# A graph transformer network of two layers on one core: the experts' shared blocks and combining put in loops, second biases added by VectorE, logits sorted in the norm, edge sums moved behind a range's first group

## The chip, the cores and the metric

One core of one Trainium2 chip runs the whole network as one program. The metric is the device time of one execution in microseconds, here the median of three. The engines are named as the profile names them: PE is TensorE's matmul side and PEld its weight loads, DVE is VectorE, ACT is ScalarE, POOL is GpSimd and SP is SyncE, which issues most of the transfers.

## The reference, cut to what matters

2500 nodes with 256 features and 80,000 directed edges go through two layers. Three pieces matter here.

- Graph convolution in both directions, then a batch norm over nodes: `h_fwd = (segment_sum(x[src], dst) / degree) @ W_l_f.T + b_l_f + x @ W_r_f.T`, `h_bwd` the same with `src` and `dst` exchanged, and the two halves of 128 features side by side.
- Mixture of experts: `shared = gelu(x @ W1s + b1s) @ W2s + b2s`; each row picks its two best of 8 logits `x @ Wr`, with softmax weights `w` normalised over the two; `routed = sum over the two of w * (gelu(x @ W1p[e] + b1p[e]) @ W2p[e] + b2p[e])`; the result is `x + shared + routed`.
- A layer norm stands before each of these stages.

The other parts (Taylor attention, linear attention, the second graph convolution, slice attention) run the same code before and after.

## The kernel before, in words

The rows are T = 20 tiles of P = 128 nodes; X (residual), XN (normed) and XT (normed and transposed) stay in on-chip memory. Every stage is a block in which each engine has its own list of instructions, joined by semaphores; all engines meet between two blocks.

**Graph stage** (`graph_stage`, from line 235). The adjacency matrix is built from one-hot matrices, 80 ranges of 32 target nodes, four ranges (x = 0 to 3) to a strip of 128 (index t). A range is a variable number of groups of four chunks of 128 edges, at least two. Per chunk DVE writes a one-hot of the keys (L505) and for three chunks of four one of the lows (L504); ACT makes the fourth low in two steps (L570, L572); PE multiplies the pair (L691). There are four one-hot buffers, so DVE may be one group ahead of PE. A range's first group stands in front of the hardware loop over the rest of its groups. Behind that loop PE turns five tiles of the strip before (`turn`, L721), sums the forward messages with them (`forward`, L730: 5 matmuls of 257 columns), and in range x = 2 multiplies the strip's own features by the root weights (L710). ACT copies that product to XN (L608), and POOL adds the bias of 256 columns to it tile by tile (L385).

**Backward stage** (`backward_stage`, from line 757). PE sums the backward messages by 7 cuts of up to three tiles (L800), from strips read back from memory. DVE combines the forward half first (`forward_h`, L882), then evacuates cut after cut (L870). PE wants the forward half at its column sums (L807), after the second cut.

**Norm before the experts** (`norm_stage("ln1")`, router given). DVE normalises 20 tiles (L157), PE transposes five blocks of four tiles (L195) into six banks and multiplies each block by the router weights (`route`, L211); all logits go to one bank. SP loads the experts' biases and the first two sets of weights meanwhile.

**Experts stage** (`experts_stage`, from line 1590). DVE copies the 160 logits of a row of partitions (L1850), takes the eight best (L1852) and their indices (L1855) tile by tile, and works out masks, counts, weights and slots. PE counts ranks by two matmuls (L1709, between hidden columns 4 and 5 of block 0). When the slots are known POOL scatters the rows to memory with 40 indirect transfers (L1684), and SP reads them back ordered by expert (L1657). Meanwhile PE computes shared blocks 0 to 2 of 512 rows: `hide`, 8 hidden columns (L1718), ACT the gelu of each (L1814), then `give`, four tiles (L1726), each followed by a matmul of the second biases `b2` with the weights of the experts (L1729, contraction over 9 rows; the weights are turned by L1702 and copied by ACT in L1807), and DVE adds the tile to X (L1881). Block 0 uses six banks for hidden columns, the other blocks two. Then PE transposes the ordered rows (L1781) and the routed tiles run in hardware loops: L1761, gelu L1827, L1767, copied by DVE in L1914 and stored by SP. When all are stored POOL gathers them by 40 indirect transfers (L1689) beside shared blocks 3 and 4, which are written out like 0 to 2, and DVE combines (L1923) and counts the next norm's statistics (L1927) in four runs of five tiles, three of them ahead of block 4's additions.

Of the kernel before, what the change touches and what calls it, by code (L numbers as in the profile page):

```python
# [19 lines left out]
def graph_network(nc, a, out):  # L20
# [44 lines left out]
    with top:  # L65
# [34 lines left out]
        def norm_stage(tag, eps=1e-5, gamma=None, beta=None, counted=0, loads=(), router=None):  # L100
# [9 lines left out]
            s_gb, s_last = sem(tag + "_gb"), sem(tag + "_last_emptied")  # L110
# [13 lines left out]
            with tmp, nc.Block() as block:  # L124
# [9 lines left out]
                def _(dve):  # L134
# [5 lines left out]

                    even, odd = lnst[:, :, 1], lnst[:, :, 4]
# [13 lines left out]
                    for b in range(NB):  # L155
# [3 lines left out]
                        if gb is not None:  # L159
# [4 lines left out]
                            dve.tensor_tensor(blk(XN, b), blk(XN, b), spread(gb[:, 1, :], 1, WT), ALU.add).then_inc(s_affine, 1)  # L164
                    dve.wait_ge(s_tr, NB * CB)
                    dve.tensor_copy(*cols(NB - 1, CB - 1)).then_inc(s_last, 1)

# [23 lines left out]
                def _(pe):  # L191
# [7 lines left out]
                    def route(b):  # L199
                        wr, arrived = router  # L200
# [7 lines left out]
                        NE = wr.shape[-1]  # L208
                        for t in range(b * WT, (b + 1) * WT):
                            for c in range(CB):  # L210
                                pe.matmul(bank[NBANK][:, t * NE:(t + 1) * NE], XT[:, c, t * P:(t + 1) * P], wr[:, c, :], start=c == 0, stop=c == CB - 1)  # L211
# [22 lines left out]
        def graph_stage(keep):  # L234
# [27 lines left out]
            s_rp, s_rc, s_rb = sem("root_product"), sem("root_copied"), sem("root_biased")  # L262
            s_fw, s_fc = sem("forward_summed"), sem("forward_copied")
            with tmp:
# [35 lines left out]
                bl = sb(tmp, "linear_bias", [P, 2 * P])  # L300
                gz = sb(tmp, "z_scale", [P, 3])
                raw = [sb(tmp, f"z_raw{k}", [P, 2, 2 * P]) for k in range(2)]
                zb, AG, back = keep
# [29 lines left out]
                with nc.Block() as block:  # L333
# [26 lines left out]
                    def _(pool):  # L360
# [263 lines left out]
                    def _(pe):  # L624
# [56 lines left out]
                        def window(i, k, x, ranges, load_next):  # L681
# [20 lines left out]
                            t = i * 2 + k  # L702
# [36 lines left out]
        def backward_stage(keep, bn, loads):  # L739
# [3 lines left out]
            zb, AG, back = keep  # L743
# [13 lines left out]
            s_var, s_rt = sem("bn_variance"), sem("bn_root")  # L757
            with tmp:
# [14 lines left out]
                with nc.Block() as block:  # L773
                    @block.sync
                    def _(sp):
# [11 lines left out]
                        sp.wait_ge(s_next, 16 * len(loads))  # L787

# [67 lines left out]
                    def _(dve):  # L856
                        st = Steps(dve, s_ch)

                        def evacuate(j):
# [3 lines left out]
                            dve.wait_ge(s_bk, j + 1)  # L863
                            st.then(dve.tensor_scalar(sd[k][:, 0:n], PS[:, 3 * k:3 * k + n, CNT:CNT + 1].rearrange("p n o -> p (n o)"), 1.0, None, ALU.max))
# [10 lines left out]
                        def forward_h():  # L875
                            st.then(dve.tensor_scalar(indeg[:, :], AG[:, :, CNT:CNT + 1].rearrange("p t o -> p (t o)"), 1.0, None, ALU.max))
# [709 lines left out]
        def experts_stage(held, arrived):  # L1586
# [12 lines left out]
            w1, w2, b1r, b2, _ = held  # L1599
# [12 lines left out]
            with tmp:  # L1612
                hid = sb(tmp, "hidden", [P, FB, W])
                b1 = sb(tmp, "b1_cols", [P, NX * FB])
                lg = sb(tmp, "logits", [P, T, NE])
                top8 = sb(tmp, "top8", [P, T, 8])
                ix = sb(tmp, "top8_index", [P, T, 8], mybir.dt.uint32)
# [5 lines left out]
                eq = [sb(tmp, f"chosen_weight{k}", [P, T, NE]) for k in range(K)]  # L1623
                mk = sb(tmp, "expert_weight", [P, T, NX])
                mkT = sb(tmp, "expert_weight_turned", [NX, NP])
# [16 lines left out]
                with nc.Block() as block:  # L1642
                    @block.sync
                    def _(sp):
# [13 lines left out]
                        sp.wait_ge(s_y, EARLY * WT)  # L1658
# [34 lines left out]
                    def _(pe):  # L1693
# [3 lines left out]
                        def hidden_bank(b, f):  # L1697
                            return bank[f % 6] if b == 0 else bank[f % 2]

                        def turn_weights(b):  # L1700
# [11 lines left out]
                        def hide(b, f, buf):  # L1712
                            if b == 0 and f >= 6:
                                pe.wait_ge(s_g, f - 5)
# [697 lines left out]
```

## Time and profile before

| | us |
|---|---|
| median of 3 executions (2136.07 to 2140.94) | 2137.51 |
| the profiled execution's own time | 2132.05 |
| its span, first to last instruction | 2130.3 |
| PE busy | 1784.7 (84%) |
| PEld busy | 1098.3 (52%) |
| DVE busy | 1084.6 (51%) |
| ACT busy | 831.9 (39%) |
| POOL busy | 260.3 (12%) |

The span is 1.75 us short of the profiled execution's own time. The busy shares are averages over stages with different limits. The mean granted clock of TensorE is 0.929 of its full 2.4 GHz; it stands at full speed or at half. The graph stage takes the first quarter of the span (to 503 us), the experts stage the part from 1008 to 1567 us.

### The profile page before, as it was taken

The numbers are of one execution on the slowest core, as the hardware profiler recorded it, in microseconds if no ns is written. First come the engines' busy times: TensorE is split into PE (matmuls) and PEld (weight loads), VectorE is DVE, ScalarE is ACT, GpSimd is POOL, SyncE is SP. The second block draws the span as 40 slices with busy tenths as digits, with TensorE's granted clock in tenths as the row PEclk, the third lists the DMA queues.
The fourth block names the chain that finished last, engine by engine and source line by source line (L and its number), as shares of the span: only waits on it lengthen the run. The fifth ranks groups of instructions, "written<-read, shape, count | busy, mean of one in ns | idle before, by whom it ended". The sixth has DMA issues, their size and how long they took to land. (4 is left out here: it accounts for less than half of the span.)

```text
span 2130.3 us, 34130 instructions
## 1 busy us (share of the span) xinstructions
PE 1784.7 (84%) x9535; PEld 1098.3 (52%) x9536; DVE 1084.6 (51%) x3108; ACT 831.9 (39%) x1831; POOL 260.3 (12%) x340
## 2 busy tenths in 40 slices
PE   6888888887858999998669999999559857976867
PEld 4234444445636423335437999997244446433436
DVE  7999988886488663334201000000347652334662
ACT  3456777773113475663112444433113233001312
POOL 2000000000092000000510000003300022201102
PEclk9999999999978999998879999999679978987988
DMA  2001111116440000002241112121110001411001
GB/s 73 0 26 60 51 75 75 75 75 212 132 138 1 1 1 1 1 1 81 77 138 40 59 60 96 59 96 56 55 40 0 0 8 67 137 64 31 0 0 51
DMA packets 87011, 117.78 MB, mean 55 GB/s; under 512 B 7404, under 2 KB 73263, under 8 KB 86927
## 3 DMA queue, kind: packets, MB, share of 16 engines
q1 hardware_dynamic: 81614, 105.62, 14.6%
q0 software_dynamic: 3936, 10.37, 1.5%
q8 instruction: 54, 0.88, 0.2%
q10 hardware_dynamic: 1376, 0.66, 0.1%
q14 instruction: 31, 0.25, 0.0%
HBM read 69.75 MB, written 46.87 MB: 55 GB/s over the span
## 5 line engine op out<-in xcount | busy, mean ns | idle before, releaser
L691 PE MATMUL bank<-onehot_key,onehot_low 128*128 128x320 bf16 x1720 | 320.3, 302 | 58.6 <-DVE onehot_key L505 23.4
L505 DVE TENSOR_SCALAR onehot_key<-iota_keys,edge_keys 128x640 bf16<-128x640 f16 x860 | 313.2, 385 | 0.0
L691 PEld LDWEIGHTS bank<-onehot_key,onehot_low 128*128 128x128 bf16 x1720 | 123.2, 97 | 241.6 <-DVE onehot_key L505 216.5
L504 DVE TENSOR_SCALAR onehot_low<-iota_low,edge_low,window_offset 128x128 bf16<-128x128 f16 x645 | 205.8, 319 | 33.0 <-PE bank L691 26.2
L1827 ACT ACTIVATE hidden<-bank,b_cols 128x128 f32<-128x128 f32 x344 | 126.5, 368 | 178.5 <-PE bank L1761 155.2
L1761 PE MATMUL bank<-slot_columns,w 128*128 x1376 | 163.6, 278 | 3.3 <-issue 3.3
L1914 DVE COPY slot_columns<-bank 128x256 f32 x43 | 18.3, 425 | 290.6 <-PE bank L1767 290.6
L1761 PEld LDWEIGHTS bank<-slot_columns,w 128*128 128x128 f32 x1376 | 163.2, 195 | 5.7 <-issue 3.5
L1767 PE MATMUL bank<-w,hidden 128*128 128x256 f32 x688 | 155.6, 379 | 0.0
L1767 PEld LDWEIGHTS bank<-w,hidden 128*128 128x128 f32 x688 | 127.4, 190 | 15.5
L570 ACT ACTIVATE low_distance<-iota_window,edge_low_negated 128x128 f32<-128x128 f32 x215 | 86.6, 403 | 112.0 <-PE bank L691 110.7
L1536 ACT ACTIVATE XT<-bank 128x512 f32<-128x512 f32 x160 | 84.5, 601 | 60.8 <-PE bank L1464 60.8
L1718 PE MATMUL bank<-XT,w 128*128 128x512 f32 x160 | 77.1, 642 | 35.2 <-ACT hidden L1814 34.6
L1881 DVE TENSOR_TENSOR X<-X,bank 128x256 f32<-128x256 f32 x20 | 8.4, 422 | 191.7 <-PE bank L1729 111.3
L1726 PE MATMUL bank<-w,hidden 128*128 128x256 f32 x320 | 79.5, 395 | 24.0 <-issue 20.7
L572 ACT ACTIVATE onehot_low<-low_distance,onesf 128x128 bf16<-128x128 f32 x215 | 86.3, 402 | 7.0
L1033 PE MATMUL bank<-sg_z,sg_strip 128*128 128x512 f16 x400 | 86.5, 379 | 1.5 <-POOL sg_z L962 1.5
L1689 POOL DMA_INDIRECT slot_columns<-slot_results,slots x40 | 38.0, 950 | 404.1 <-SPq L1670 392.2
L1726 PEld LDWEIGHTS bank<-w,hidden 128*128 128x128 f32 x320 | 60.6, 194 | 44.3 <-issue 30.8
L1408 ACT ACTIVATE XT<-bank 128x512 f32<-128x512 f32 x120 | 62.9, 599 | 27.5 <-PE bank L1358 27.5
L1993 PE MATMUL bank<-w_kv,la_cols 128*128 128x512 f32 x160 | 73.0, 601 | 0.0
L1718 PEld LDWEIGHTS bank<-XT,w 128*128 128x128 f32 x160 | 32.7, 209 | 76.2 <-issue 39.7
(475 smaller groups left out, 2870.3 us busy)
## 6 DMA issues: line engine op xcount, KB each, us to landing
AT_dram<-at_strip SPq DMA_DIRECT2D x20, 640.0 KB, 4.0
A_dram<-a_strips SPq DMA_DIRECT2D x20, 640.0 KB, 3.0
sg_strip<-AT_dram SPq DMA_DIRECT2D x20, 640.0 KB, 3.9
back_strip<-A_dram SPq DMA_DIRECT2D x24, 480.0 KB, 7.0
w<-in_L_ffn_W1p SPq DMA_DIRECT2D x8, 1024.0 KB, 4.9
w<-in_L_ffn_W2p SPq DMA_DIRECT2D x8, 1024.0 KB, 7.6
slot_rows<-ty_zero SPq DMA_DIRECT2D x1, 6144.0 KB, 23.7
slot_columns<-slot_rows SPq DMA_DIRECT2D x12, 512.0 KB, 8.9
```

What stands on the lines that cost most here:

```text
L504: dve.tensor_scalar(ohl[:, q, :], iow[:, :], lowc[:, ds(c, 1)], woff[:, ds(w, 1)], ALU.subtract, ALU.is_equal)
L505: dve.tensor_scalar(ohk[:, q, :], ioh[:, :], key[:, ds(c, 1)], None, ALU.is_equal).then_inc(s_key[q], 1)
L570: act.activation(far[:, q - QV, :], wide[:, :], ACT.Square, bias=lows[:, ds(chunk(n, offset, q), 1)]).then_inc(s_sq, 1)
L572: act.activation(ohl[:, QV:Q, :], far[:, 0:Q - QV, :], ACT.Relu, bias=onesf[:, 0:1], scale=-1.0).then_inc(s_low, 1)
L691: last = pe.matmul(bank[2 * (x % 2) + h][:, 0:HB], ohl[:, q, :], ohk[:, q, h * HB:(h + 1) * HB], start=start and q == 0, stop=q == Q - 1, ...
L1033: last = pe.matmul(bank[5 + d % 3][:, :], strips[d % NBUF][:, s, :], zb[:, s, :], start=s == 0, stop=s == T - 1)
L1536: act.activation(FE[:, m % NF, :], bank[m % NS][:, :], ACT.Square).then_inc(p_fa, 1)
L1718: last = pe.matmul(hidden_bank(b, f)[:, :], w1[buf][:, c, f * P:(f + 1) * P], XT[:, c, b * W:(b + 1) * W], start=c == 0, stop=c == CB - 1)
L1726: pe.matmul(bank[2 + j][:, 0:C], hid[:, f, j * P:(j + 1) * P], w2[buf][:, f, :], start=f == 0, stop=False)
L1761: last = pe.matmul(bank[f % 4][:, 0:P], w1[buf][:, c, f * P:(f + 1) * P], XS[:, t, c * P:(c + 1) * P], start=c == 0, stop=c == CB - 1)
L1767: last = pe.matmul(bank[4][:, 0:C], hid[:, f, 0:P], w2[buf][:, f, :], start=f == 0, stop=f == FB - 1)
L1827: act.activation(hid[:, f, 0:P], bank[f % 4][:, 0:P], ACT.Gelu, bias=b1[:, ds((e + 1) * FB + f, 1)]).then_inc(s_rg, 1)
```

## The change

1. Graph stage: for x = 1, 2, 3 the `forward` sums of the strip before are issued behind the range's first group and ahead of the loop over its other groups, no longer behind `turn`; for x = 0 they stay where they were. POOL's bias additions are taken out.
2. Backward stage: POOL adds the backward half of the bias by cuts (7 instructions), for each of which DVE's evacuation waits; DVE adds the forward half in one instruction of 128 x 2560 at the head of `forward_h`.
3. Norm: logits of a block go to one of two banks; DVE copies, sorts and indexes them block by block (`sort`), blocks 0 to 2 ahead of its last copy of XT, blocks 3 and 4 behind it, inside the norm's block.
4. Experts: b2 is loaded to all partitions (9 x 256 values each, where it was 9 rows). The masks of weights, their turning, their copies and the 20 bias matmuls are gone. DVE adds the shared second bias to all of X in one instruction, and each routed tile's second bias as it evacuates it (in a loop over experts around the loop over tiles).
5. Experts: the rank matmuls stand ahead of block 0, behind a wait for the counts. Shared blocks 0 to 2 and 3 to 4 are hardware loops on PE, ACT and DVE with six banks for hidden columns; columns 2 to 5 wait for the additions of the block before, columns 6 and 7 for gelus of this block. Combining is a loop over tiles: add the first, wait, add the second, wait, statistics.

```diff
@@ graph_stage, PE
                             group(before, True)
                             following = load_next()
+                            t = i * 2 + k
+                            if t >= 1 and x:
+                                forward(t - 1, 1 - k, x)
                             with pe.Fori(before + 1, following[0]) as n:
                                 group(n, False)
                             if t >= 1:
                                 turn(t - 1, 1 - k, x)
-                                forward(t - 1, 1 - k, x)
+                                if x == 0:
+                                    forward(t - 1, 1 - k, x)
@@ graph_stage, POOL
-                        for t in range(T):
-                            pool.wait_ge(s_rc, t + 1)
-                            pool.tensor_tensor(XN[:, t, :], XN[:, t, :], bl[:, :], ALU.add).then_inc(s_rb, 1)
@@ backward_stage
+                    @block.gpsimd
+                    def _(pool):
+                        for lo, hi in cuts:
+                            pool.tensor_tensor(part(XN, 1, slice(lo, hi)), part(XN, 1, slice(lo, hi)), spread(bl[:, P:2 * P], 1, hi - lo), ALU.add).then_inc(s_bias, 1)
...
+                            dve.wait_ge(s_bias, j + 1)
...
+                            dve.tensor_tensor(part(XN, 0), part(XN, 0), spread(bl[:, 0:P], 1, T), ALU.add)
@@ norm_stage, DVE
+                    def sort(b):
+                        lg, top8, ix = router[2]
+                        NE = lg.shape[-1]
+                        dve.wait_ge(s_lg, b + 1)
+                        dve.tensor_copy(lg[:, b * WT:(b + 1) * WT, :].rearrange("p t e -> p (t e)"), bank[NBANK + b % 2][:, 0:WT * NE]).then_inc(s_lc, 1)
+                        dve.wait_ge(s_lc, b + 1)
+                        for t in range(b * WT, (b + 1) * WT):
+                            last = dve.max(top8[:, t, :], lg[:, t, :])
+                        st.then(last)
+                        for t in range(b * WT, (b + 1) * WT):
+                            last = dve.max_index(ix[:, t, :], top8[:, t, :], lg[:, t, :])
+                        if b == NB - 1:
+                            st.then(last)
@@ experts_stage, PE
+                        def shared(blocks, buf, arrived, routed_tiles=None):
+                            with pe.Fori(*blocks) as b:
+                                if routed_tiles is not None:
+                                    pe.wait_ge(s_rc, routed_tiles + 1)
+                                pe.wait_ge(s_w[buf], arrived)
+                                for f in range(FB):
+                                    if 2 <= f < 6:
+                                        pe.wait_ge(s_yf, b * WT + (f - 1))
+                                    if f >= 6:
+                                        pe.wait_ge(s_g, b * FB + (f - 5))
+                                    for c in range(CB):
+                                        last = pe.matmul(bank[f % 6][:, :], w1[buf][:, c, f * P:(f + 1) * P], XT[:, c, ds(b * W, W)],
+                                                         start=c == 0, stop=c == CB - 1)
+                                    last.then_inc(s_h, 1)
+                                pe.wait_ge(s_g, b * FB + FB)
+                                for j in range(WT):
+                                    for f in range(FB):
+                                        last = pe.matmul(bank[2 + j][:, 0:C], hid[:, f, j * P:(j + 1) * P], w2[buf][:, f, :],
+                                                         start=f == 0, stop=f == FB - 1)
+                                    last.then_inc(s_y, 1)
...
+                        pe.wait_ge(s_cnt, 3)
+                        pe.wait_ge(s_bt, 1)
+                        for k, m in enumerate((below, onesf)):
+                            last = pe.matmul(bank[6 + k][:, 0:NE * T], m[:, :], cnt[:, :, :].rearrange("p e t -> p (e t)"), start=True, stop=True)
+                        last.then_inc(s_rank, 1)
+                        shared((0, EARLY), 0, 32)
@@ experts_stage, DVE
+                        st.then(dve.tensor_tensor(X[:, :, :], X[:, :, :], spread(b2[:, 0, :], 1, T), ALU.add))
+                        shared((0, EARLY))
...
+                        with dve.Fori(0, NE) as e:
+                            first, end = bounds(dve, e)
+                            with dve.Fori(first, end) as t:
+                                dve.wait_ge(s_ry, t + 2)
+                                dve.tensor_tensor(XS[:, t, :], bank[4][:, 0:C], b2[:, ds(e + 1, 1), :].rearrange("p o c -> p (o c)"), ALU.add).then_inc(s_rc, 1)
 
                         def combine(g):
                             dve.wait_ge(s_gat[g], 16 * K * GG)
...
+                            with dve.Fori(g * GG, (g + 1) * GG) as t:
+                                dve.wait_ge(s_yf, t + (WT + 1))
+                                for k in range(K):
+                                    dve.scalar_tensor_tensor(out=X[:, t, :], in0=XS[:, t + k * T, :], scalar=d[:, 2 + k, ds(t, 1)], in1=X[:, t, :],
                                                              op0=ALU.mult, op1=ALU.add).then_inc(s_cmb, 1)
+                                    dve.wait_ge(s_cmb, t * K + (k + 1))
                                 dve.bn_stats(lnst[:, t, :], X[:, t, :])
```

## Rows read from the trace of the kernel before

**Rows 1.** Stages: stretch, length, busy us (instructions) by engine, clock, DMA share, GB/s

```profile
300.00:400.00 100.00, 85.67 (x620) 49.01 (x620) 89.68 (x321) 74.20 (x171) 4.56 (x6) 1.00 0.20 80
```

**Rows 2.** Waits of DVE, 130 to 503 us: total, times, longest

```profile
DVE onehot_low L504 <- PE bank L691: 26.2, 34, 0.9
```

**Rows 3.** Timeline, graph stage: start, us, engine, line, operation, count, [idle before, releaser]

```profile
317.69 0.48 PEld L730 LDWEIGHTS bank<-z_halves,at_strip 128*128 128x128 f16 x5
...
318.19 0.73 PEld L710 LDWEIGHTS bank<-wr,XT 128*128 128x128 f32 x4
...
319.85 0.32 DVE L504 TENSOR_SCALAR onehot_low<-iota_low,edge_low,window_offset 128x128 bf16<-128x128 f16 x1 [0.88 <-PE bank L691]
...
320.38 0.80 DVE L504 TENSOR_SCALAR onehot_low<-iota_low,edge_low,window_offset 128x128 bf16<-128x128 f16 x1
320.40 0.73 POOL L385 TENSOR_TENSOR XN<-XN,linear_bias 128x256 f32<-128x256 f32 x1 [16.63 <-ACT XN L608]
```

**Rows 4.** Timeline, head of the backward stage

```profile
507.24 10.72 DVE L882 SCALAR_TENSOR_TENSOR XN<-forward_sums,forward_scale,XN 128x128 f32<-128x128 f32 x40
...
525.19 4.24 PE L807 MATMUL bank<-XN,onesf 128*128 128x512 f32 x10
```

**Rows 5.** Groups: line, engine, operation, xcount | busy, mean ns | idle before

```profile
L1914 DVE COPY slot_columns<-bank 128x256 f32 x43 | 18.3, 425 | 290.6 <-PE bank L1767 290.6
...
L1214 POOL TENSOR_TENSOR X<-X,bproj 128x1024 f32<-128x1024 f32 x5 | 11.7, 2346 | 0.0
...
L164 DVE TENSOR_TENSOR XN<-XN,ln2b_gb 128x1024 f32<-128x1024 f32 x5 | 6.1, 1225 | 0.2
```

**Rows 6.** Timeline, end of the norm and hidden columns of block 0

```profile
1001.15 6.83 PE L211 MATMUL bank<-router,XT 128*128 128x8 f32 x32
...
1008.43 10.68 PE L1718 MATMUL bank<-XT,w 128*128 128x512 f32 x20
...
1014.04 0.20 DVE L1858 TENSOR_TENSOR top_weights<-top 128x20 f32<-128x20 f32 x1
...
1015.43 0.44 DVE L1867 TENSOR_TENSOR chosen_count<-chosen 128x160 f32<-128x160 f32 x1
...
1019.49 5.31 PE L1718 MATMUL bank<-XT,w 128*128 128x512 f32 x12
1019.69 0.33 DVE L1886 COPY chosen_count<-bank 128x160 f32<-128x160 f32 x1 [2.31 <-PE bank L1709]
...
1024.56 1.25 POOL L1684 DMA_INDIRECT slot_rows<-XN,slots  x1 [15.64 <-DVE slots L1905]
```

**Rows 7.** Timeline beside the scatter, and the end of blocks 0 to 2

```profile
1038.40 3.32 PEld L1726 LDWEIGHTS bank<-w,hidden 128*128 128x128 f32 x16 [0.33 <-issue]
...
1042.68 1.04 PE L1702 MATMUL bank<-ident,expert_weight 128*9 128x128 f32 x8
...
1067.59 0.59 ACT L1807 ACTIVATE expert_weight_turned<-bank 9x512 f32<-9x512 f32 x1 [41.11 <-remote]
...
1074.44 1.10 POOL L1684 DMA_INDIRECT slot_rows<-XN,slots  x1 [0.30 <-issue]
...
1081.73 13.32 PE L1718 MATMUL bank<-XT,w 128*128 128x512 f32 x24 [34.57 <-ACT hidden L1814]
...
1145.73 10.47 PEld L1781 LDWEIGHTS bank<-ident,slot_columns 128*128 128x128 f32 x96 [0.92 <-DVE X L1881]
```

**Rows 8.** Timeline beside the gather and to the stage's end

```profile
1465.64 14.00 PE L1718 MATMUL bank<-XT,w 128*128 128x512 f32 x32 [0.62 <-DVE slot_columns L1914]
...
1516.73 0.95 POOL L1689 DMA_INDIRECT slot_columns<-slot_results,slots  x1 [0.30 <-issue]
...
1523.18 0.42 DVE L1881 TENSOR_TENSOR X<-X,bank 128x256 f32<-128x256 f32 x1 [33.92 <-DMA A_dram<-a_strips]
...
1526.37 16.30 PE L1718 MATMUL bank<-XT,w 128*128 128x512 f32 x32
...
1561.00 4.04 DVE L1923 SCALAR_TENSOR_TENSOR X<-slot_columns,top_weights,X 128x256 f32<-128x256 f32 x10
```

More of the change, by code:

```diff
@@ L164, in _ @@
                             dve.tensor_tensor(blk(XN, b), blk(XN, b), spread(gb[:, 1, :], 1, WT), ALU.add).then_inc(s_affine, 1)
+                    if router is not None:
+                        for b in range(NB - 2):
+                            sort(b)
                     dve.wait_ge(s_tr, NB * CB)
                     dve.tensor_copy(*cols(NB - 1, CB - 1)).then_inc(s_last, 1)
+                    if router is not None:
+                        sort(NB - 2)
+                        sort(NB - 1)
                 @block.scalar
@@ L208, in route @@
                         NE = wr.shape[-1]
+                        if b >= 2:
+                            pe.wait_ge(s_lc, b - 1)
                         for t in range(b * WT, (b + 1) * WT):
                             for c in range(CB):
-                                pe.matmul(bank[NBANK][:, t * NE:(t + 1) * NE], XT[:, c, t * P:(t + 1) * P], wr[:, c, :], start=c == 0, stop=c == CB - 1)
+                                k = t - b * WT
+                                last = pe.matmul(bank[NBANK + b % 2][:, k * NE:(k + 1) * NE], XT[:, c, t * P:(t + 1) * P], wr[:, c, :], start=c == 0, stop=c == CB - 1)
+                        last.then_inc(s_lg, 1)
                     for b in range(NB):
@@ L739, in backward_stage @@
         def backward_stage(keep, bn, loads):
-            zb, AG, back = keep
+            zb, AG, back, bl = keep
             factor, vec = bn
@@ L1705, in count_ranks @@
-                        def count_ranks():
-                            pe.wait_ge(s_cnt, 3)
-                            pe.wait_ge(s_bt, 1)
-                            for k, m in enumerate((below, onesf)):
-                                last = pe.matmul(bank[6 + k][:, 0:NE * T], m[:, :], cnt[:, :, :].rearrange("p e t -> p (e t)"), start=True, stop=True)
-                            last.then_inc(s_rank, 1)
-                        def hide(b, f, buf):
-                            if b == 0 and f >= 6:
-                                pe.wait_ge(s_g, f - 5)
-                            if b and f >= 2:
-                                pe.wait_ge(s_g, b * FB + (f - 1))
-                            for c in range(CB):
-                                last = pe.matmul(hidden_bank(b, f)[:, :], w1[buf][:, c, f * P:(f + 1) * P], XT[:, c, b * W:(b + 1) * W],
-                                                 start=c == 0, stop=c == CB - 1)
-                            last.then_inc(s_h, 1)
@@ L1722, in give @@
-                        def give(b, j, buf):
-                            if b:
-                                pe.wait_ge(s_yf, (b - 1) * WT + (j + 1))
-                            for f in range(FB):
-                                pe.matmul(bank[2 + j][:, 0:C], hid[:, f, j * P:(j + 1) * P], w2[buf][:, f, :], start=f == 0, stop=False)
-                            if j == 0:
-                                pe.wait_ge(s_mc, b + 1)
-                            pe.matmul(bank[2 + j][:, 0:C], mkT[:, b * W + j * P:b * W + (j + 1) * P], b2[:, :], start=False, stop=True).then_inc(s_y, 1)
@@ L1871, in _, with shared @@
                         st.then(dve.tensor_tensor(d[:, 3, :], d[:, 1, :], d[:, 2, :], ALU.mult))
[L1872 to L1881 removed]
+                        def shared(blocks):
+                            with dve.Fori(*blocks) as b:
+                                for j in range(WT):
+                                    dve.wait_ge(s_y, b * WT + (j + 2))
+                                    dve.tensor_tensor(X[:, b * WT + j, :], X[:, b * WT + j, :], bank[2 + j][:, 0:C], ALU.add).then_inc(s_yf, 1)
                         dve.wait_ge(s_rank, 1)
@@ L1934, in _ @@
+                        for g in range(T // GG - 1):
+                            combine(g)
+                        shared((NB - 1, NB))
                         combine(T // GG - 1)
```

142 lines of the change are left out of this document (33 added, 109 removed).

## The prediction, made before the changed kernel was run

> **What bounds the kernel now.** I read the page's engine shares first, then the span in slices, the table of stretches, the waits of DVE, and last the timeline of the stages that the diff touches. The profiled execution took 2132.05 us, 5.5 below the median shown; sums are made against it and 5.5 is added at the end.
>
> Graph stage (to 503 us): DVE is busy 89.7 of 100 us, PE 85.7, ACT 74.2, at full clock [rows 1]. DVE is the bound, and from 130 to 503 us it waits 34 times for PE's one-hot products, 26.2 us in all, at most 0.9 [rows 2]. The reader is to see such a wait (0.88) behind five matmuls of `forward` and the root weights, and right after it a DVE operation of 0.32 us stretched to 0.80 beside POOL's bias addition of 0.73 [rows 3].
>
> Experts stage (1008 to 1567 us): PE is the bound except at two places. Beside the scatter PE idles 34.6 us until 1081.7, because ACT's gelus don't come; ACT copies masks at 1067.59 from a product that PE had finished at 1043.7. PE resumes some 6 us after the last indirect transfer ends at 1075.5, and slowly: 24 matmuls in 13.32 us, where 32 take 14.0 at the start of block 3; I read it as a clock at the half of its two levels (1.2 GHz) for the first of them, after the idle time [rows 7, 8]. Beside the gather, DVE waits 33.9 us for a tile until 1523.18, 5.5 us after the last issue's end (1516.73 + 0.95); PE starts block 4 at 1526.37 [rows 8]. Hides of block 3 (14.0 us) and four tiles (about 4 x 4.28) would have ended at 1497: some 29 us are lost there. What the two places share is POOL's indirect transfers.
>
> **Graph stage.** (a) POOL's 20 additions go. Each stretches a DVE operation by 0.80 - 0.32 = 0.48 [rows 3]: 20 x 0.48 = -9.6 us; bounds 0 (only one row shown is stretched, others might fall into idle time) and -14.6 (20 x 0.73). (b) `forward` between two ranges took 318.19 - 317.69 = 0.50 us of PE's stream [rows 3]. Moved behind the first group it stands where DVE has four chunks of lead, and the burst that DVE waits behind is 0.5 shorter. 34 waits x 0.5 = 17 us at most; a wait may be shorter than that, and ACT, busy 74 of 100, is the next to be late: I take -12.5. The other end: 57 moved sums, each now inside the one-hot stream, could hold DVE back 0.5 each, +28; I stay near the first because a first group is followed by further groups, with PE only 86% busy. All of DVE's idle time, 10.3 of 100 us [rows 1] over some 370 us, would be -38 for both. Sum -22.
>
> (c) Backward: the new DVE addition of 128 x 2560 costs, by 1.225 us for 1024 columns, 3.1 us [rows 5]. `forward_h` then ends at 518.0 + 3.1 = 521.1, and PE wants it at 525.2 [rows 4]: 0. POOL's seven additions of up to 384 columns, by 2.346 for 1024, are 0.9 us each, beside it; if DVE lost all their time (6 us) the end would be 527, +2. The Trainium skill ("SBUF — State Buffer", Terms) says that DVE and GpSimd share a port pair held for a whole instruction, and the loser fully blocks. The stretched row agrees (0.80 for 0.32); by it the backward term would be that +2 instead of 0.
>
> **Norm and slots.** (d) Blocks 0 to 2 are sorted while DVE waits for PE. Logits end at 1007.98 (1001.15 + 6.83) [rows 6]; the last block's sort is about a fifth of the 5.7 us now spent from the stage's start to 1014.04, with its own wait 1.4: the stage starts 1.4 later, 1009.7. Counts are ready 1.83 us after the first weights operation (1014.04 to 1015.87) and a start of 1 us: 1012.7. The ranks' four matmuls at half clock are through at 1013.9; only then do hides begin, against 1008.4 now. From PE's ranks to slots it is 4.9 us (1019.69 to 1024.56) [rows 6]: the scatter starts at 1018.8, not 1024.6, and ends at 1069.8.
>
> (e) Blocks 0 to 2. Hides of block 0 take 10.68 + 5.31 = 16.0 [rows 6], to 1029.9; gelu 0.8; a tile is now 4.28 from loads to the next thing (1038.40 to 1042.68), of which the loads are 3.32 [rows 7]. Without the bias matmul I take 3.42, so 13.7 for four: 1044.4. Block 1's hides run to column 5 with six banks, then stall as now, until about 5.4 behind the scatter's end: 1075.2. Then two columns (3.4) and 3 for the half clock, 0.8, 13.7: 1096.1. Block 2: 13.9 + 0.8 + 13.7 = 28.4, 1124.5; routed transposes at 1125.2 against 1145.73 [rows 7]: -20.5. The terms inside: scatter 5.7 earlier, four columns of block 1 before the stall (6.9), 12 bias matmuls (8 behind it, 6.9). Adding b2 to X (20 tiles, some 5.4 us of DVE) lies under the hides, and the masks gone save DVE as much. b2's load grows to 1.2 MB, and PE needs nothing of it before the first routed tile. Ends: +5 (all of (d) late, no earlier scatter) and -44 (no stall at all).
>
> Routed tiles: addition instead of copy, and DVE idles 290.6 us over 43 tiles beside 0.425 each [rows 5]: 0, with 6.8 us of cover per tile.
>
> (f) Blocks 3 and 4. From the start at 1465.64 the end of combining is at +101.1 (1561.00 + 4.04 + 1.73 for statistics = 1566.8). The gather runs as before, the stall ends at about +57.5 to +58.5, block 4 takes 2.3 (half clock) + 28.4 = 30.7: +89.3. Behind the last addition the loop adds the last five tiles. Now ten additions take 4.04 and five statistics 1.73 [rows 8], 1.15 per tile; in the loop each addition waits for its own end, I take 1.75: 8.7, +98.5, so -2.6. Fifteen tiles before cost 26 us beside block 4's 31: covered, barely. Ends: -35 (no stall), and the third rival below.
>
> Sum: -9.6 - 12.5 - 20.5 - 2.6 = -45; 2132 - 45 + 5.5 = 2093 us.
>
> **Rivals.**
> 1. *The stalls belong to the straight-line code, not to the transfers.* PE's own matmuls, which wait for nothing, come one by one in the gather (29 us lost). Were the written-out code the reason, loops would end both: -44 and -35 with the graph's -22 give -101, 2036. For it: 43 routed tiles run in loops without a gap beyond PE's own [rows 5]. Against: ACT and DVE, with few instructions, are late too, and both stalls end 5 to 6 us after the last transfer [rows 7, 8]. A half of it (one stall goes) gives about 2069.
> 2. *The graph stage gives only POOL's part or less* (ACT's one-hots become late): -10 or 0, so 2105 to 2115. For it: ACT's 74%. Against: the longest DVE wait stands exactly behind the burst [rows 3].
> 3. *Slower: the combining loop sets the end.* With a price p per tile on DVE, the stage ends at about +60.5 + 20p once p exceeds 1.9; all 42 us of the other gains are eaten at 20p = 40.6 + 42, p = 4.1 us, and the kernel is then at 2140 or more. Against: 1.15 us per tile now, and two waits for own results; routed loops show DVE on time. The Trainium skill ("Runtime: NRT & Kernel Launch", Instruction fetch mechanics) speaks for it: a taken branch can break the prefetch of instructions, and unrolling is preferred. The routed loops' rows don't agree, their tiles have no gap.
>
> **How the numbers follow.** Forecast 0.57 (2093, by itself 2080 to 2108), both stalls gone 0.14, one gone 0.15, graph gain missing 0.08, slower 0.06. Range 2050 to 2116: it holds the forecast, one stall gone and the graph rival, and leaves out 0.14 below and 0.06 above. A measurement tells a change of over 0.2%, 4.3 us: faster 0.91, same 0.03 (between rivals 2 and 3), slower 0.06.
>
> **What would show it.** (a) no DVE one-hot above 0.4 us; (b) DVE's waits for PE from 130 to 503 us near 13 us, and the stage's end near 481 for 503; (c) `forward_h` ending before PE's column sums; (d) the first indirect scatter 9 to 10 us after the stage's start, where it is 16 now; (e) PE idle beside the scatter, 25 to 30 us, ending some 5 us behind the last transfer: no such idle time is rival 1; (f) the same beside the gather, and the last five tiles at 1.75 us each. I am wrong if the graph stage ends after 495, or if either stall is gone or grows.

## The result

The changed kernel takes 2106.79 us (median of 4), the kernel before 2136.79 in the same series: ratio 0.9859, 95% interval 0.9833 to 0.9885, 30 us gained. The prediction was 2093, 44 us gained; its range, 2050 to 2116, holds the time. The forecast's direction stood, and so did the mechanism of its largest terms; the gain was a third smaller than forecast. Beside that the runs brought something that no profile ahead of them could show: the two long stalls beside the indirect transfers, on which half of the sum was built, appear in some series of runs and not in others; each series ran on one chip. Where they are absent the gain is 19 us (2047.51 against 2066.93, ratio 0.9907, 0.9885 to 0.9930).

### The profile page after: what moved, and what is told of

The parts are those of the page before. It is cut to its first block and busy times, and to the rows that moved or that the text cites. A ratio compares the mean times of both kernels' runs of the same rounds, so it can differ in the third digit from the quotient of the medians.

```text
span 2107.2 us, 34421 instructions
## 1 busy us (share of the span) xinstructions
PE 1776.1 (84%) x9475; PEld 1096.6 (52%) x9476; DVE 1094.0 (52%) x3110; ACT 830.2 (39%) x1828; POOL 258.6 (12%) x327
## 5 line engine op out<-in xcount | busy, mean ns | idle before, releaser
L1890 DVE TENSOR_TENSOR slot_columns<-bank,b_rows 128x256 f32 x43 | 18.3, 425 | 289.3 <-PE bank L1759 289.3
L1735 PE MATMUL bank<-XT,w 128*128 x160 | 82.0, 655 | 21.5 <-issue 18.8
L1855 DVE TENSOR_TENSOR X<-X,bank 128x256 f32 (+1 forms) x20 | 8.1, 420 | 161.9 <-DMA X<-in_x 103.4
L1741 PEld LDWEIGHTS bank<-w,hidden 128*128 128x128 f32 x320 | 61.8, 194 | 44.8 <-issue 29.1
L215 PE MATMUL bank<-ident,XN 128*128 128x128 f32 x160 | 31.3, 371 | 46.2 <-DVE XN L171 27.7
```

The source lines that it names most:

```text
L1735: last = pe.matmul(bank[f % 6][:, :], w1[buf][:, c, f * P:(f + 1) * P], XT[:, c, ds(b * W, W)], start=c == 0, stop=c == CB - 1)
L1741: last = pe.matmul(bank[2 + j][:, 0:C], hid[:, f, j * P:(j + 1) * P], w2[buf][:, f, :], start=f == 0, stop=f == FB - 1)
```

## The profile after

The profiled execution took 2108.92 us (span 2107.2), in which all stages before the edge loop started 2.8 us later than in the profile before. The table sets the terms beside each other; each is taken between two marks of PE, so that what came earlier drops out.

| term | forecast | measured | marks (before; after) |
|---|---|---|---|
| graph stage (a, b) | -22 | -19.0 | first to last one-hot product: 50.31 to 497.85; 53.13 to 481.68 |
| backward stage (c) | 0 | +3.2 here, about +1.5 in the mean | last one-hot product to next stage's first matmul: 88.2 and 88.7; 91.4 here, 88.3 to 91.1 in the eleven other profiles with this stage |
| last sort (d) | +1.4 | +1.6 | logits' end to stage start: 0.30; 1.86 |
| stage head and blocks 0 to 2 (d, e) | -20.5 | -12.8 | logits' end to the transposes: 137.75; 124.97 |
| routed tiles | 0 | -1.2 | first transpose to the first hide of block 3: 319.90; 318.73 (318.6 to 320.0 in seven other profiles, so nothing clear) |
| blocks 3 and 4, combining (f) | -2.6 | +0.4 | first hide of block 3 to last statistics: 101.1; 101.5 |

(The fourth row contains the third.) The other stages run the same code and drifted by up to 5 us either way between profiles: a second pair has spans of 2134.6 and 2103.4, 31 apart, where this one has 23.

**Graph.** Waits of DVE in the one-hot stage, after (total, times, longest), which answer to [rows 2]:

```profile
DVE onehot_low L524 <- PE bank L711: 11.5, 25, 0.6
DVE onehot_low L524 <- issue: 9.2, 32, 0.4
```

and the stretch that answers to [rows 1], same columns:

```profile
300.00:400.00 100.00, 90.94 (x649) 51.02 (x647) 91.21 (x336) 77.76 (x180) 0.00 (x0) 1.00 0.20 80
```

DVE's wait for PE fell by 14.7 us, and the longest wait by 0.3 (0.9 to 0.6), about half of the 0.5 of the moved burst. DVE makes 336 instructions in 100 us instead of 321; POOL makes none. But 4.7 us came back as "issue", waits for nothing shown, so the saved wait was not saved whole. From 100 us on the kernel before has exactly 20 one-hots of DVE, lows and keys, that take 0.72 to 0.85 us, and the changed kernel none above 0.45: the single stretched row of [rows 3] stood for all twenty. One more of them, before:

```profile
338.00 0.79 POOL L385 TENSOR_TENSOR XN<-XN,linear_bias 128x256 f32<-128x256 f32 x1 [16.87 <-ACT XN L608]
338.13 0.85 DVE L505 TENSOR_SCALAR onehot_key<-iota_keys,edge_keys 128x640 bf16<-128x640 f16 x1
```

**Backward.** Timeline at the stage's head, after (it answers to [rows 4]):

```profile
491.38 9.12 POOL L816 TENSOR_TENSOR XN<-XN,linear_bias 128x384 f32<-128x384 f32 x7 [435.76 <-POOLq L356]
...
492.38 3.63 DVE L906 TENSOR_TENSOR XN<-XN,linear_bias 128x2560 f32<-128x2560 f32 x1
...
497.87 12.61 DVE L913 SCALAR_TENSOR_TENSOR XN<-forward_sums,forward_scale,XN 128x128 f32<-128x128 f32 x40
...
511.41 4.24 PE L836 MATMUL bank<-XN,onesf 128*128 128x512 f32 x10
```

The addition took 3.63 us (forecast 3.1), and `forward_h`, 10.72 before, 12.61 beside POOL's additions. It ended at 510.5. PE's column sums began at 511.41, 15.9 us after PE's first product, where that was 15.0. The row shows no idle time before them: PE came straight from its own products, and `forward_h` was still 0.9 us ahead. The 0.9 us that PE lost lie in its first cut (9.4 us for 8.6, at a mean granted clock of 0.71 for 0.78). Three of the other profiles, of e1, e2 and the second paused run, do show PE waiting there for `forward_h`, by 0.2 to 0.7 us. The rule of the Trainium skill that the prediction weighed ("SBUF — State Buffer", Terms: the loser of the shared port pair blocks) agrees with `forward_h` growing beside POOL, but the +2 that the prediction set beside it did not reach PE in this profile. The rest of the row's +1.5 lies ahead of PE's first product (12.3 and 12.6 us after the last one-hot before, 11.9 to 13.9 after) and behind the sums; its cause is open.

**Ranks first, and the scatter.** Timeline at the experts stage's head, after (it answers to [rows 6]):

```profile
998.09 0.90 PE L1767 MATMUL bank<-chosen_count,rows_below 128*128 128x160 f32 x2 [2.57 <-DVE chosen_count L1845]
...
999.32 15.61 PE L1735 MATMUL bank<-XT,w 128*128 x32
...
1004.14 5.48 DVE L1881 TENSOR_TENSOR X<-X,b_rows 128x5120 f32<-128x5120 f32 x1
1004.53 6.21 POOL L1710 DMA_INDIRECT slot_rows<-XN,slots  x1 [8.72 <-DVE slots L1879]
...
1011.04 0.97 POOL L1710 DMA_INDIRECT slot_rows<-XN,slots  x1 [0.31 <-issue]
```

Logits end at 993.31, so hides start 6.0 us behind them (forecast 5.9) and the scatter 11.2 (forecast 10.8). Then comes what was not forecast: the first transfer lasts 6.21 us and not 1.25, because it meets DVE's addition of the second bias to all of X. The 5.4 us by which the scatter starts earlier are gone, and it ends at 1060.43, 67.1 behind the logits, where it was 67.6.

**The stall beside the scatter**, after (it answers to [rows 7]):

```profile
1053.33 1.01 PE L1735 MATMUL bank<-XT,w 128*128 x1 [2.49 <-issue]
...
1059.34 1.09 POOL L1710 DMA_INDIRECT slot_rows<-XN,slots  x1 [0.30 <-issue]
...
1066.10 1.28 ACT L1808 ACT_TABLE_LOAD   x1 [50.45 <-DMA X<-in_x]
...
1066.62 7.59 PE L1735 MATMUL bank<-XT,w 128*128 x12 [1.78 <-DVE X L1855]
...
1118.28 10.47 PEld L1779 LDWEIGHTS bank<-ident,slot_columns 128*128 128x128 f32 x96 [1.02 <-DVE X L1855]
```

PE doesn't stop as before, it trickles: one matmul of block 1 every 1.4 to 3.5 us, waiting for nothing that is shown. ACT, idle for 50 us, has had products ready since 1031, so some 35 of them are the stall's. Both resume 6 us behind the last transfer, as before (1081.73 against 1075.54). The start follows the number of transfers more than the time: in all six profiles with stalls, at the scatter and at the gather, 18 to 22 have begun at PE's first idle time over 0.6 us that isn't the 0.78 between a block's hides and its tiles. That is 22 to 25 us after the first transfer's start, but 28 to 32 where the first takes 6.21. Why, no run shows.

**Combining**, after (it answers to [rows 8]): first and second tile of fifteen, block 4's additions, and the last five tiles.

```profile
1497.02 0.48 DVE L1897 SCALAR_TENSOR_TENSOR X<-slot_columns,top_weights,X  x1 [0.18 <-DVE X L1855]
1497.77 0.48 DVE L1897 SCALAR_TENSOR_TENSOR X<-slot_columns,top_weights,X  x1 [0.27 <-DVE X L1897]
1498.41 0.43 DVE L1900 BATCH_NORM_STATS2 lnst<-X  x1
1499.01 0.48 DVE L1897 SCALAR_TENSOR_TENSOR X<-slot_columns,top_weights,X  x1 [0.18 <-issue]
...
1527.54 1.40 DVE L1855 TENSOR_TENSOR X<-X,bank 128x256 f32<-128x256 f32 x4
1528.85 0.48 DVE L1897 SCALAR_TENSOR_TENSOR X<-slot_columns,top_weights,X  x1
...
1538.11 0.43 DVE L1900 BATCH_NORM_STATS2 lnst<-X  x1
```

A tile costs 1.99 us (1497.02 to 1499.01), 1.15 before. Fifteen take 30.5 us, and block 4's last tile, which PE finished at 1525.68, is added late: all four additions come in a row from 1527.54, and the last five tiles begin 3.2 us behind PE's last product, where that was 0.4. The last five take 9.7 us.

## The experiments

**e1: the forward sums back.** The changed kernel without its move of `forward`:

```diff
-                            if t >= 1 and x:
-                                forward(t - 1, 1 - k, x)
                             with pe.Fori(before + 1, following[0]) as n:
                                 group(n, False)
                             if t >= 1:
                                 turn(t - 1, 1 - k, x)
-                                if x == 0:
-                                    forward(t - 1, 1 - k, x)
+                                forward(t - 1, 1 - k, x)
```

> The changed kernel with its forward sums back behind turn; POOL's additions stay out. The graph stage's one-hot part took 447.5 us of the span before (from 50.3 to 497.9) and 428.6 after (53.1 to 481.7): 19 gained. Theory: half of it is the moved sums, so this kernel is 9 to 10 us slower than the changed one (some 2116), DVE waits for PE's products over 20 us again, and the one-hot part takes 438. Rival: all of the gain is POOL's additions going, then this kernel stands within 3 us of the changed one, with the one-hot part at 429 to 431.

2055.8 us, ratio to before 0.9944 (0.9924 to 0.9963), on a chip on which the kernel before takes 2066.59. The one-hot part takes 439.1 us (53.01 to 492.15), 10.6 more than in the changed kernel (428.6) and 8.4 less than before (447.5). DVE's waits, same columns as above:

```profile
DVE onehot_low L524 <- PE bank L711: 25.1, 34, 0.9
...
DVE onehot_low L524 <- issue: 6.6, 25, 0.3
```

The waits for PE are those of [rows 2] again, within 1.1 us. So the moved sums are worth 10.6 us (forecast 12.5), POOL's additions 8.4 (forecast 9.6). The comparison across chips holds here, since this part takes 447.5 and 447.3 us in the two profiles before and 427.8 to 429.1 in all eleven with the moved sums, on every chip.

**e2: the second bias of X added later.** The line `X += b2` stands behind DVE's copies of the transposed rows, ahead of the routed tiles.

> The changed kernel with DVE's addition of the shared second bias to all of X moved behind its copies of the transposed rows, ahead of the routed tiles. In the changed kernel the first indirect transfer lasted 6.21 us beside that addition of 5.48, where it lasts 1.25 before. Theory: the addition keeps POOL from writing its first transfer, the scatter ends 5 us late and PE's stall with it; so here the first transfer takes 1.3, the scatter ends 51 us after its start and not 56, and the kernel is 5 us faster, some 2102. Rival: the stall ends by something else than the scatter's end; then the first transfer is short, and the time stays at 2107.

2044.43 us, ratio 0.9890 (0.9859 to 0.9922). The first transfer, in this kernel:

```profile
1004.62 1.25 POOL L1710 DMA_INDIRECT slot_rows<-XN,slots  x1 [8.72 <-DVE slots L1879]
...
1029.73 13.90 PE L1735 MATMUL bank<-XT,w 128*128 x32
```

1.25 instead of 6.21: the addition was what held it. In all nine profiles with the addition there (the changed kernel's own among them) the first transfer took 6.21, in the three without it 1.25. PE did not stall here: block 1 follows block 0 at once (1029.73), beside 40 transfers in a row. So this run can't say what the addition costs beside a stall. Without one it costs nothing at the transposes: they start 94.3 us behind the logits here and in e1, which has the addition.

**e3 and e4: rows of transfers broken up, and halved.** e3 waits in the scatter after 12 transfers for block 0's additions and after 26 for block 1's; in the gather likewise. e4 makes only the first of each two, so it leaves out half of the routed rows.

```diff
                         for t in range(T):
                             n = P if t < T - 1 else LAST
+                            if t == 6:
+                                pool.wait_ge(s_yf, WT + WT)
+                            if t == 13:
+                                pool.wait_ge(s_yf, WT + 2 * WT)
... (the gather likewise)
```

> The changed kernel with two pauses in each series of 40 indirect transfers: in the scatter after 12 for block 0's additions, and after 26 for block 1's; in the gather after 12 for block 3's additions, and after 26 for block 4's second tile. Both stalls set in some 23 us after the first transfer, that is after 18. Theory: something fills up over a row of transfers and empties when POOL rests, so with rows of 12 to 14 no stall comes: routed transposes start some 30 us earlier, the stage ends some 50 us earlier, 2055 to 2065 in all. Rival one: what slows the engines is the issuing itself, once some 18 have gone, however far apart; then PE stalls in the second or third group, and the time is 2100 or more, later by the pauses. Rival two: the stall belongs to a place in the engines' code (the back branch of the shared loop, a table load of ACT); then it stands at the head of block 1 as now.

> The changed kernel with only the first of the two rows of each node scattered and gathered: 20 indirect transfers in a row, not 40; the second rows are left out, so the output is not the reference's. Theory: the stall sets in after 18 transfers and ends 5 to 6 us behind the last, so here it is at most 8 us long at both places, and the stage is some 25 us shorter at each, 2055 to 2065. Rival: the stall is set by code or by a time, and 25 fewer us of transfers don't take it away: PE is idle for over 20 us at one of the places.

e3: 2058.53 us, ratio 0.9966 (0.9946 to 0.9986); e4: 2045.78 (one run). Neither stalled, but neither did e1 and e2 with their 40 in a row, on the same chip. So both expectations go untested: the runs say nothing of the stall. e3 shows the price of the pauses alone: +2.7 us at the transposes (their rows come back late) and +9.8 at the stage's end, where the gather's end now decides.

**The same kernels again, beside each other.**

> The changed kernel, unaltered, beside the kernel before on the chip of this series. In the first series both stalls beside the indirect transfers were absent on the chip used, with all 40 transfers of each kind in a row. Theory: the stalls belong to the chip or its surroundings, not to the code: without them the changed kernel takes 2046 to 2050 on such a chip, and its gain over the kernel before is 20 us or so (graph stage 18, experts the rest). Rival: the stalls come and go from run to run, then the runs of this kernel spread by 30 us or more.

> The kernel before, unaltered, for its profile on this chip. Theory: where the changed kernel shows no stall, this one shows none: PE goes from block 0 to block 1 without a pause, the stage's first three blocks end some 35 us earlier than in the profile shown of before, and blocks 3 and 4 some 28 us earlier. Rival: this kernel stalls and the loops cured the changed one.

On this chip the changed kernel takes 2105.82 (before 2138.19; 0.9854, 0.9838 to 0.9871), and both stall. PE in the kernel before, block 1:

```profile
1082.98 3.78 PE L1718 MATMUL bank<-XT,w 128*128 128x512 f32 x4 [35.67 <-ACT hidden L1814]
```

The time forecast there, 2046 to 2050, was for a chip without stalls and missed by 56 us. The rival, stalls that come and go from run to run, is out: the four runs lie within 5.3 us, and no series mixes the two. The theory, that stalls belong to the chip or its surroundings, is what is left; since each chip was seen in one series only, chip and time can't be told apart. Gaps of PE over 0.7 us, summed beside scatter and gather, in all kernels with 40 transfers: before 34.6 and 23.2, before again 35.7 and 25.0, changed 21.8 and 24.2, changed again 26.5 and 25.2; on the chip of e1 and e2 2.3 or less at each place. (Up to three gaps of 0.78 between a block's hides and its tiles, which every profile has, can be in such a sum.)

**e6: the shared blocks written out.** `pe.Fori`, `act.Fori` and `dve.Fori` over blocks become plain loops of the program that writes the code.

> The changed kernel with its shared blocks written out on PE, ACT and DVE (the three loops over blocks undone, nothing else). Theory: a loop over blocks costs nothing that ends late, so this kernel is within 2 us of the changed one, either way, with the same clock. Rival (a taken branch breaks the prefetch of instructions): this kernel is faster by more than 3 us, and in the changed one PE has a gap of over 1 us at each block's head. Other rival (loops hold the instructions close and so avoid the stalls): PE stalls beside the transfers here and not in the changed kernel, 25 us or more.

2108.60 us, ratio 0.9856 (0.9840 to 0.9873), the changed kernel's 0.9854 beside it. That is 2.8 us more than the changed kernel, where at most 2 were expected, but the intervals lie over each other: neither a cost nor a saving of the loops shows. The stall is that of the changed kernel, before and after its longest gap:

```profile
1052.85 1.01 PE L1735 MATMUL bank<-XT,w 128*128 128x512 f32 x1 [1.79 <-issue]
...
1068.80 3.78 PE L1735 MATMUL bank<-XT,w 128*128 128x512 f32 x4 [14.94 <-DVE X L1855]
```

24.8 us of gaps in all, 26.5 in the changed kernel on the same chip (longest 15.04). Rival 1 of the prediction, stalls of the straight-line code, is refuted from both sides: loops stall as written-out code does.

**e5: combining written out, bias later.** The bias line moves as in e2, and:

```diff
-                            with dve.Fori(g * GG, (g + 1) * GG) as t:
-                                dve.wait_ge(s_yf, t + (WT + 1))
-                                for k in range(K):
-                                    dve.scalar_tensor_tensor(...).then_inc(s_cmb, 1)
-                                    dve.wait_ge(s_cmb, t * K + (k + 1))
-                                dve.bn_stats(lnst[:, t, :], X[:, t, :])
+                            for k in range(K):
+                                for t in range(g * GG, (g + 1) * GG):
+                                    if not k:
+                                        dve.wait_ge(s_yf, t + (WT + 1))
+                                    if k:
+                                        dve.wait_ge(s_cmb, t + g * GG + 1)
+                                    dve.scalar_tensor_tensor(...).then_inc(s_cmb, 1)
+                            for t in range(g * GG, (g + 1) * GG):
+                                dve.wait_ge(s_cmb, t + (g + 1) * GG + 1)
+                                dve.bn_stats(lnst[:, t, :], X[:, t, :])
```

> The changed kernel with the combining written out as before (ten additions, then five statistics, in four runs of five tiles), and the second-bias addition of X behind the copies of the transposed rows. In the changed kernel a tile of the loop costs DVE 1.97 to 2.25 us against 1.15 before, block 4's additions come 2 us late behind 15 tiles of it, and the last five take 10 us. Theory: written out, the stage ends 5 to 6 us earlier than in the changed kernel (2 of late additions, 4 of the last five tiles). Rival: the gather's end bounds the last five tiles, and under 2 us are gained.

2099.33 us, ratio 0.9814 (0.9788 to 0.9839), 6.5 less than the changed kernel on the same chip (2092.9 to 2103.9 for 2105.1 to 2110.5). The stage's end:

```profile
1524.66 0.42 DVE L1855 TENSOR_TENSOR X<-X,bank 128x256 f32<-128x256 f32 x1 [3.03 <-PE bank L1741]
1524.99 4.04 DVE L1900 SCALAR_TENSOR_TENSOR X<-slot_columns,top_weights,X 128x256 f32<-128x256 f32 x10
1528.95 1.72 DVE L1904 BATCH_NORM_STATS2 lnst<-X 128x6 f32<-128x256 f32 x5
```

From block 3's first hide to the next norm's transposes it is 5.3 us less (99.97 for 105.24), within the forecast 5 to 6. With the bias away the scatter ends 5 us earlier, but the transposes come only 2.3 earlier after the logits (123.4 for 125.7; 1.5 against the first profile of the changed kernel). PE where it resumes, in e5 and then in the changed kernel on the same chip:

```profile
1060.81 12.41 PE L1735 MATMUL bank<-XT,w 128*128 x24 [0.39 <-issue]
...
1064.54 8.42 PE L1735 MATMUL bank<-XT,w 128*128 x12 [15.04 <-DVE X L1855]
```

Behind the logits (993.87 and 991.30) PE resumes 6 us sooner, with 24 of block 1's 32 matmuls still to do where the changed kernel has 12. The reason is in the same traces: the nineteenth transfer, too, comes 5 us sooner, and PE slows 24 us after the first and not 29, already among block 0's tiles, which take 22.8 us for 14.1.

**The last three runs.**

> The kernel of e3_paused once more (12, 14 and 14 transfers with pauses for PE's progress between), for a chip on which the stalls appear: of three series so far two had them in every profile (PE idle 21 to 36 us beside the scatter and 23 to 25 beside the gather) and one had them in none. On such a chip, theory: something fills up over some 18 transfers in a row and empties in a pause; then the idle times are under 8 us, and the kernel is at 2065 to 2075 against 2106. Rival: the pauses don't matter, PE is idle over 20 us at one of the places at least. On a chip without stalls (the kernel before near 2067) this run tells only the cost of the pauses, as e3_paused did.

> The kernel of e4_half once more (20 transfers in a row in place of 40; the second row of each node is left out, so the output is not the reference's). On a chip with stalls, theory: the stall sets in after some 18 transfers and ends 5 to 6 us behind the last, so PE idles under 10 us at each place. Rival: it is not the row's length that counts, and PE idles 20 us or more at one of them. On a chip without stalls it repeats e4_half.

> The kernel of e5 (combining written out, X's second bias added later) with the two pauses of e3 in the scatter alone. The stalls have come on two chips and stayed away on two others, for one and the same kernel. On a chip with stalls, theory of filling and emptying: the stall beside the scatter is gone, the kernel is 22 to 28 us faster than e5 there (2099), 2071 to 2077, and the stall beside the gather (24 us) stays. Rival: PE is idle over 20 us beside the paused scatter, and the time is 2098 to 2105. On a chip without stalls: the pauses cost 2.7 us (the rows come back late for the transposes), the combining gives 6, so 2041 to 2046 for the changed kernel's 2045.

> The changed kernel, unaltered. On a chip without stalls (the kernel before near 2067): 2044 to 2048, ratio 0.989 to 0.991, that is 20 us gained, graph stage 18 of them; on one with stalls 2106, ratio 0.985, as twice before.

None met a chip with stalls (two further chips). The paused kernel took 2056.58 (0.9946, 0.9929 to 0.9962) and the halved one 2046.42. The changed kernel took 2047.51 beside a kernel before at 2066.93 (0.9907, 0.9885 to 0.9930), as expected; the best version, e7, took 2038.68 (0.9863, 0.9842 to 0.9883), a little better than its forecast, though its pauses cost 3.5 us at the transposes: its combining, written out, ends 63.5 us behind block 3's first hide, the changed kernel's beside it 71.0, a gain of 7.5 for the 6 that were expected. It beats both kernels where there is no stall; e5 does so where there is one. Whether pauses, or half as many transfers, end a stall stays open: neither was tried on a chip that has it.

## Why the prediction came out as it did

1. (a) and (b), -22: right, 3 us too large. -9.6 became -8.4 and -12.5 became -10.6, each shown by one run against two. One stretched row times 20 was sound: there are twenty. The burst was 34 waits x 0.5 less a share that was taken, not worked out; the wait for PE fell by 13.6 us between e1 and the changed kernel (0.4 for each of 34), and 2.6 came back as "issue". That 12.5 came so near 10.6 is in part luck.
2. (c), 0: the stage takes about 1.5 us more in the mean, with a spread of 3 between profiles. The slack between `forward_h` and PE was 7.2 us and is 0.9: 3.6 went to the addition, 1.9 to the longer `forward_h`, 1.9 to the small operations ahead of it, beside POOL; PE's own delay of 0.9 gave some back. The prediction named the first and bounded the rest. That `forward_h` ends before the column sums, its sign for (c), came true here, and PE waited in three other profiles, by 0.7 at most; no more than that of the 1.5 is shown to come from it.
3. (d): within half a microsecond for the stage's start, the hides and the scatter's start. Its last mark failed: the scatter ends 67.1 behind the logits for a forecast 61.8.
4. (e), -20.5 against -12.8: one sentence that failed is "Adding b2 to X ... lies under the hides". It did, on DVE and PE; but it stood beside POOL's first transfer, which took 6.21 and not 1.25. PE resumed 73.3 us behind the logits for a forecast 67.2: 5.0 of that, 0.4 for the scatter's start and 0.8 for a later restart (6.2 behind the last transfer, not 5.4). Another 1.2 are block 1, of which five columns and not six were done by then, and 0.5 the tiles (3.52 us each for 3.42). The other sentence is "Block 1's hides run to column 5 with six banks, then stall": banks don't set the stall's start here. where the stalls are, PE's own instructions slow once some 19 transfers have begun, and the five columns were done only because the long first transfer put that off and the trickle went on for 33 us. In e5, with the first transfer at 1.25 and the scatter's end within half a microsecond of the forecast (62.2 for 61.8), two columns were done and the transposes came 123.4 behind the logits for the forecast 117.2. So the addition accounts for some 2 of the 7.7 us, and the pace of block 1 beside the transfers for most of the rest.
5. (f), -2.6 against +0.4: the size of the combining tile, 1.75 taken, 1.99 measured and up to 2.2 for some of the fifteen. Fifteen tiles then no longer fit beside block 4 ("covered, barely"): they take 30.5 us, and block 4 29.5 (1496.17 to 1525.68). e5 undoes it for 5.3 us. This was rival 3's mechanism at half its threshold of 4.1 us.
6. Stalls: that they stay, and end 5 to 6 us behind the last transfer, was right in the series of the prediction (6.2 and 4.3). "What the two places share is POOL's indirect transfers" is true but not the cause by itself: on other chips the same 40 transfers stall nobody. The loops are not the cause either (e6). What on a chip decides is open. So the total owes something to luck: half of the sum was built on stalls, and the series had them. On a chip without, the changed kernel takes 2047.5 us, just below the range, and the kernel before 2067.

Without stalls the gain is 19.4 us, about what the graph stage alone gives (-19 + 1.5). The bias matmuls saved on PE (3.0 us a block: from block 2's first hide to the transposes it is 29.4 for 32.4, so 15 for five blocks) are for the most part given back by the ranks put first (5.6) and the combining loop (7.5, e7 against the changed kernel). That sum is argued, not shown: no profile of the kernel before was taken on such a chip.

## What to carry to other kernels

A moved instruction is to be held against every engine that runs beside its new place, not only its own: a 5.5 us addition hidden from DVE and PE delayed a queue of transfers by 5.0. And its price is known only from the run without it: 5.0 us by the marks were about 2 at the transposes. A loop that waits for each of its own results pays for it on every turn, here 0.84 us on top of 1.15, and is cheap only while cover lasts; how much of that is the loop and how much the waits wasn't separated. And before half of a forecast is built on a stall, a second profile of the unchanged kernel on another chip tells whether the stall is the kernel's own.

## What the runs showed of the hardware

In two series (the first, and that of e5 and e6; whether on one chip or two is not known) PE has 21 to 36 us of gaps beside the scatter and 23 to 25 beside the gather, in all six profiles; on the three chips of the other series none has them, in eight profiles (five of these with pauses or half of the transfers); the kernel before differs by 71 us between them (2138.2 and 2066.9). Each chip was seen in one series only. Where there are stalls, PE slows when 18 to 22 transfers of a row have begun, to one matmul in 1.4 to 3.5 us at the scatter, and ACT starts nothing for some 35 us with products ready; the transfers themselves keep their pace of 1.27 us.

A DVE addition of 128 x 5120 with both inputs in on-chip memory (5.48 us) holds POOL's indirect transfer: 6.21 us in nine profiles, 1.25 in the five without the addition there, the two of the kernel before among them. A POOL addition of 128 x 256 stretches a one-hot of DVE beside it from 0.32 to 0.80 us or from 0.38 to 0.85, eighteen times of twenty; the first two take 0.72 and 0.73.
